# Linear attention in a five-stage network: scores within halves of 64 tokens, a state per half, weighted sums as one run of 64-row tiles

## What is computed

```python
q = softplus(x @ Wq.T + bq); k = softplus(x @ Wk.T + bk); v = x @ Wv.T + bv   # 16 heads of width 8
kv = cumsum(k[:, :, :, None] * v[:, :, None, :], axis=1)    # over the tokens
k1 = cumsum(k, axis=1)
num = einsum('zsD,zsDe->zse', q, kv);  den = sum(q * k1, axis=-1)
out = (num / den) @ Wo.T + bo
```

## Time and profile before

| what | value |
|---|---|
| three runs | 1309.18, 1315.74, 1320.01 us; median 1315.74 |
| span of the profiled execution, first to last instruction | 1294.8 us |
| the runs above this span | by 14.4 to 25.2 us (the profiled execution has no time of its own beside its span) |
| busy, share of the span | PE 83%, ACT 62%, DVE 50%, PEld 39%, POOL 29% |
| the linear stage | from the first scores at 844.9 us to the first expert loads at 1090.9 us |

### The profile page before, as it was taken

How to read it: one execution, slowest core, us unless ns; L and a number is a source line. 1 busy time by engine, 2 the same in 40 slices (tenths; PEclk the granted TensorE clock), 3 DMA queues, 4 the chain that set the end, 5 groups by cost and what they waited for, 6 DMA issues and landing times. The chain is left out here.

```text
span 1294.8 us, 21020 instructions
## 1 busy us (share of the span) xinstructions
PE 1070.8 (83%) x7616; PEld 500.4 (39%) x7616; DVE 653.5 (50%) x2099; ACT 807.3 (62%) x1164; POOL 373.6 (29%) x376
## 2 busy tenths in 40 slices
PE   4479998999999999999978858888877986998940
PEld 3242222322222231232256535534544554665620
DVE  5762555366356332333156326657867684633522
ACT  4348787877898989999934525555544441464520
POOL 2100110211110102333010664144331165265435
PEclk8679998999999999999998979989888897998975
DMA  5270370027028500300011323200000011233422
GB/s 144 55 105 1 58 101 2 1 41 106 14 42 120 157 1 15 114 17 18 19 38 49 104 83 94 68 17 20 15 14 5 1 34 58 72 109 110 133 66 67
DMA packets 83796, 74.08 MB, mean 57 GB/s; under 512 B 11440, under 2 KB 77872, under 8 KB 82800
## 3 DMA queue, kind: packets, MB, share of 16 engines
q1 hardware_dynamic: 73900, 54.93, 19.2%
q0 software_dynamic: 8192, 16.79, 4.4%
q10 hardware_dynamic: 1604, 0.99, 0.3%
HBM read 39.26 MB, written 33.42 MB: 56 GB/s over the span
## 5 line engine op out<-in xcount | busy, mean ns | idle before, releaser
L1275 ACT ACTIVATE attn_probs<-ps 128x1024 f32<-128x1024 f32 x512 | 485.5, 1072 | 73.1 <-PE ps L986 73.0
L1003 PE MATMUL ps<-attn_probs,attn_v 128*18 128x512 f32 x2048 | 274.9, 610 | 6.3 <-DVE room L1234 5.6
L1641 POOL DMA_INDIRECT slots<-moe_xr,moe_slot x128 | 124.8, 975 | 184.4 <-ACT attn_probs L1275 82.7
L986 PE MATMUL ps<-stack 50*128 50x512 bf16 x1024 | 166.2, 389 | 7.2 <-issue 1.2
L1651 POOL DMA_INDIRECT moe_back<-results,moe_slot x128 | 123.3, 963 | 115.2 <-PE ps L1696 45.4
L1706 PE MATMUL ps<-stack,lin_scores 128*128 x312 | 153.1, 613 | 0.0
L1807 ACT ACTIVATE lin_scores<-ps 128x256 f32<-128x256 f32 x156 | 58.5, 382 | 114.9 <-PE ps L1706 114.8
L986 PEld LDWEIGHTS ps<-stack 50*128 50x128 bf16 x1024 | 34.0, 94 | 244.1 <-ACT attn_probs L1275 229.3
L1780 DVE TENSOR_TENSOR lin_scores<-ps,lin_scores 128x256 f32<-128x256 f32 x156 | 59.1, 419 | 104.6 <-ACT lin_scores L1807 104.5
L1732 PE MATMUL ps<-stack,lin_scores 128*128 x624 | 85.1, 280 | 4.8 <-ACT lin_heads_out L1820 4.8
L1732 PEld LDWEIGHTS ps<-stack,lin_scores 128*128 128x128 f32 x624 | 77.4, 195 | 6.5 <-issue 6.5
(11 more groups left out here) (237 smaller groups left out, 1552.1 us busy)
## 6 DMA issues: line engine op xcount, KB each, us to landing
moe_gathered<-slots SPq DMA_DIRECT2D x76, 128.0 KB, 2.3
results<-lin_heads_out SPq DMA_DIRECT2D x76, 128.0 KB
stack<-qk_parts SPq DMA_DIRECT2D x36, 256.0 KB, 8.9
slots<-zeros SPq DMA_DIRECT2D x2, 2496.0 KB, 15.2
qk_parts<-moe_xr SPq DMA_DIRECT2D x32, 128.0 KB, 2.7
qk_parts<-moe_xr SPq DMA_DIRECT2D x16, 192.0 KB, 2.8
stack<-in_expert_w SPq DMA_DIRECT2D x1, 3072.0 KB, 10.4
stack<-qk_parts SPq DMA_DIRECT2D x12, 192.0 KB, 10.6
```

The source lines that it names most:

```text
L986: instruction = T.matmul(k.ps[:, SCORE_BANKS[i % 3][s], :], d.stack[b % 2][rows, 1, pair, kt * P:(kt + 1) * P], d.stack[b % 2][rows, 0, pa ...
L1003: instruction = T.matmul(k.ps[32 * j:32 * j + STRIP, PV_BANK, :], d.v[:, b % 2, kt, first:first + STRIP], d.probs[:, n % A_PROBS, j * BANK ...
L1275: A.activation(d.probs[:, n % A_PROBS, 2 * e * BANK:2 * (e + 1) * BANK], k.ps[:, banks[0]:banks[1] + 1, :].rearrange("p a n -> p (a n)"), ...
L1641: G.indirect_dma_start(out=k.dram["slots"][half], out_offset=bass.IndirectOffsetOnAxis(ap=d.slot[:, s, at, c:c + 1], axis=0), in_=d.xr[:, ...
```

## The change

Each chunk is cut into two halves s = 0, 1 of 64 tokens. Scores are made within a half only: 64 x 64 for a head, 256 columns for a head group, eight matmuls in place of four, each in a tile of 32 rows by 64 columns. The product that hides the later tokens has 256 columns. DVE reads the two banks 0 and 1 by one instruction, ACT the banks 2 and 3 by one. Each half needs its own state before it: `lstate` sums k x (v, 1) over the tokens 0 to 63 and over all 128 of the chunk, for all 32 chunks, DVE adds the total of the chunk before to both, and POOL spreads both to 288 columns. In `ldiv` the product with the state becomes two, one for each half, with a row of zeros in the first half of a sequence. The weighted sums of a chunk are 32 matmuls of 9 x 64 in tiles of 64 rows by 32 columns, in one run; half s writes bank 4 + s, and one ACT instruction copies both. `ldiv` comes two steps after them.

```diff
@@ plan_linear @@
-            if gr == HEAD_GROUPS - 1 and (u + 1) % TPB:
-                state = ("lstate", u)
+            if gr == 0:
+                state = ("lstate", g * TPG + c)
...
-        if n >= L_LAG and L_STEPS[n - L_LAG][2] == HEAD_GROUPS - 1:
+        if n >= L_LAG and n % HEAD_GROUPS == 0:
             sums = (n - L_LAG) // HEAD_GROUPS
-            works.insert(0, list(linear_finish(sums)))
+        if n >= L_LAG and n % HEAD_GROUPS == DIVIDE_AT:
+            works.insert(0, list(linear_finish((n - L_LAG) // HEAD_GROUPS)))
@@ pe_linear_side, lstate @@
+            for s, tokens in enumerate((slice(0, SUB), slice(0, P))):
+                for gr in range(HEAD_GROUPS):
+                    rows, heads = slice(32 * gr, 32 * (gr + 1)), slice(gr * HPG, (gr + 1) * HPG)
+                    instruction = T.matmul(k.ps[rows, bank, s * HPG * VW:(s + 1) * HPG * VW], d.k_tok[tokens, gg % NQ, c, rows],
...
@@ pe_linear_side, ldiv @@
+            T.wait_ge(k.l_state, u + 1)
+            for s in range(2):
...
+                instruction = T.matmul(k.ps[s * SUB:(s + 1) * SUB, bank, 0:HEADS * VW], d.q[:, gg % NQ, at:at + SUB], before,
+                                       start=True, stop=False)
@@ pe_linear, scores @@
+        for gr in range(HEAD_GROUPS // 2, HEAD_GROUPS):
+            T.matmul(k.ps[:, gr, 0:SUB_SCORES], d.hide[:, :], d.later[:, :, :].rearrange("p j t -> p (j t)"), start=True,
+                     stop=False)
         for gr in range(HEAD_GROUPS):
             rows = slice(32 * gr, 32 * (gr + 1))
-            T.matmul(k.ps[:, gr, :], d.k[rows, g % NQ, tokens],
-                     d.qz[rows, g % NQ, c, :, :].rearrange("p j t -> p (j t)"), start=not gr % 2,
-                     stop=True).then_inc(k.full[gr], 1)
+            for s in range(2):
+                at = c * P + s * SUB
+                instruction = T.matmul(k.ps[s * SUB:(s + 1) * SUB, gr, 0:SUB_SCORES], d.k[rows, g % NQ, at:at + SUB],
+                                       d.qz[rows, g % NQ, 2 * c + s, :, :].rearrange("p j t -> p (j t)"),
+                                       start=gr < HEAD_GROUPS // 2, stop=True)
+        instruction.then_inc(k.l_scored, 1)
@@ pe_linear, weighted_sums @@
-        for j in range(HPG):
-            instruction = T.matmul(out[PAD * j:PAD * j + VW, :], d.v[:, g % NQ, c, gr * HPG + j, :],
-                                   d.scores[:, n % NS, j * P:(j + 1) * P], start=True, stop=True)
+        for gr in range(HEAD_GROUPS):
+            for j in range(HPG):
+                for s in range(2):
+                    rows = slice(s * SUB, (s + 1) * SUB)
+                    instruction = T.matmul(k.ps[PAD * j:PAD * j + VW, L_OUT[s], gr * SUB:(gr + 1) * SUB],
+                                           d.v[rows, g % NQ, c, gr * HPG + j, :],
+                                           score_rows(d, u)[rows, gr, j * SUB:(j + 1) * SUB], start=True, stop=True)
         instruction.then_inc(k.l_av, 1)
@@ pool_linear_side, lstate @@
+            G.tensor_tensor(d.state[:, u % NST, :, :].rearrange("p s (g n) -> p s g n", g=HEAD_GROUPS),
+                            d.total[:, u % NST, :, :][:, :, None, :].broadcast_to(spread_to),
...
```

More of the change, by code:

```diff
@@ L415, in plan_linear @@
                 before.append(("lnorm", prepared + 1))
-            u = g * TPG + c
-            u = g * TPG + c
-            if gr == HEAD_GROUPS - 1 and (u + 1) % TPB:
-                state = ("lstate", u)
+            if gr == 0:
+                state = ("lstate", g * TPG + c)
         fill(before)
-        if n < len(L_STEPS) and gr == 0:
-            for i in range(HEAD_GROUPS):
-                k.banks.fill(("lscore", n + i), i)
         if state:
@@ L1994, in take, with scores @@
         return pe_take(T, k, key)
-    def scores(n, g, c):
+    def scores(u):
+        g, c = divmod(u, TPG)
         if c == 0:
@@ L2000, in scores @@
             T.wait_ge(k.l_masked[1], g + 1)
-        tokens = slice(c * P, (c + 1) * P)
-        for gr in range(HEAD_GROUPS):
-            bank = take(("lscore", n + gr))
-            if gr % 2:
-                T.matmul(k.ps[:, bank, :], d.hide[:, :], d.later[:, :, :].rearrange("p j t -> p (j t)"), start=True,
-                         stop=False)
+        if u:
+            T.wait_ge(k.l_read[0], u)
+            T.wait_ge(k.l_read[1], u)
+        for gr in range(HEAD_GROUPS // 2, HEAD_GROUPS):
+            T.matmul(k.ps[:, gr, 0:SUB_SCORES], d.hide[:, :], d.later[:, :, :].rearrange("p j t -> p (j t)"), start=True,
+                     stop=False)
@@ L2028, in pe_linear @@
     T.wait_ge(k.l_v_one, 1)
+    for bank in range(HEAD_GROUPS):
+        T.wait_ge(k.free[bank], k.banks.after["loop1"][bank])
     for piece in k.l_first:
@@ L2035, in pe_linear @@
         if n < len(L_STEPS) and n % HEAD_GROUPS == 0:
-            scores(n, *L_STEPS[n][:2])
+            scores(n // HEAD_GROUPS)
+        if k.l_sums[n] is not None:
+            weighted_sums(k.l_sums[n])
         if state:
@@ L2204, in act_linear @@
             side(piece)
-        for m in (n + 1, n + 3) if n < len(L_STEPS) and n % HEAD_GROUPS == 0 else ():
-            bank, fill = k.use["lscore", m]
-            A.wait_ge(k.full[bank], fill + 1)
-            A.activation(d.scores[:, m % NS, :], k.ps[:, bank, :], ACT_FN.Relu).then_inc(k.free[bank], 1)
+        if n < len(L_STEPS) and n % HEAD_GROUPS == 0:
+            u = n // HEAD_GROUPS
+            A.wait_ge(k.l_scored, u + 1)
+            A.activation(score_rows(d, u)[:, 2:4, :], k.ps[:, 2:4, 0:SUB_SCORES], ACT_FN.Relu).then_inc(k.l_read[1], 1)
+        if k.l_sums[n] is not None:
+            u = k.l_sums[n]
+            A.wait_ge(k.l_av, u + 1)
+            A.activation(d.sums[:, u % 2, :].rearrange("p (g s t) -> p s g t", g=HEAD_GROUPS, s=2),
+                         k.ps[:, L_OUT[0]:L_OUT[1] + 1, 0:SUB_SCORES].rearrange("p s (g t) -> p s g t", g=HEAD_GROUPS),
+                         ACT_FN.Copy).then_inc(k.l_sums_out, 1)
         for piece in after:
```

107 lines of the change are left out of this document (53 added, 54 removed).

## The result

The changed kernel takes 1310.8 us, median of 17 runs (1303.6 to 1313.0), beside 1315.9 for the kernel before, median of 17 timed beside it: ratio 0.9956, 95% interval 0.9942 to 0.9971. The forecast was 1297, a gain of 18.7 us; the measured gain is 5 to 6. Sign right, size wrong by 13 us. The profiled execution took 1303.6 us, with a span of 1301.8; so a run's time is its span and 1.8 us. That alone says something of the profile of before: its span of 1294.8 belongs to an execution of 1296.6 us, 19 us under the median beside it and under every one of the 17. The profiled execution of the changed kernel is also the fastest of its 17, 7 us under their median, so a difference of two spans is not the gain of the medians.

The account below looks back on a forecast made before the run. PE was taken to set the pace before the scatters and POOL after; 7.87 - 1.11 + 0.4 = 7.16 us a chunk gives -21.3 us, POOL +3.1, together -18, so 1297 us against 1315.7; eight-in-ten range 1283 to 1320.

Parts of the forecast that it names:

- the last one 53 us later: Predicted sign in the linear stage: first scatter near 1018 instead of 1039.8, last scatter 53 us after it.
- Rival C: PE in the linear stage: instructions don't come fast enough at 118 records a chunk; some +58 us, 1374 us; chance 5%.
- The sign by which I would call the forecast wrong: First scatter later than 1030, or second stretch over 6 us longer because POOL waits for late totals.
- Weighted sums: PE, first stretch: 64 records with row halves side by side take 0.7 us for 1.53, -0.83 us a chunk.
- Scores: PE, first stretch: 256 columns in eight tiles take 0.81 us for 1.29, -0.48 us a chunk.
- The state: PE, first stretch: two runs of 64 and 128 rows, the second waiting for the first, +0.28 us a chunk.
- item 7: PE, first stretch: new waits for ACT's copies before ldiv, lz and lproj, less old waits, net +0.4 us a chunk.
- rival E: PE idles more, so its clock falls to 0.80 and work costs 0.6 us more a chunk; 1312 us; chance 5%.
- Item 8: POOL, second stretch: seven state products of 288 columns at 0.87 us for six of 144, +3.1 us.
- Rivals A: PE's two halves take turns instead of running together, so the work hardly falls; 1318 us; chance 15%.
- B (a least time of 25 ns a record): Each PE record holds the array 25 ns, so weighted sums cost +0.32 us a chunk; 1316 to 1325 us; chance 7%.
- D (the new waits at +1.1): PE, first stretch: new waits and DVE's bursts eat the gain, +1.1 us a chunk; 1315 us; chance 15%.

Follow-up runs that it names:

- e14: The changed kernel, unedited, profiled again on a chip where the kernel before takes 1295.38 us: 1286.94 us (one run).
- e16: The changed kernel, unedited, on a chip where the kernel before takes 1298.98 us: 1278.82 us, ratio 0.9844 to before.
- e1: The kernel before, unedited, profiled once more: 1321.65 us, span 1319.8.
- e6: The changed kernel with three extra dense products of 256 columns ahead of each of PE's waits: 1307.80 us, ratio 0.9919 to before.
- e12: The kernel before with three extra dense products of 256 columns ahead of the same PE waits: 1320.88 us, ratio 0.9994 to before.
- e13: The changed kernel with four small 64-column products in place of each large one of e6: 1289.45 us, ratio 0.9942 to before.
- e17: The kernel of e6 (changed, three extra products ahead of PE's waits) timed on the chip of e16: 1271.02 us, ratio 0.9794 to before.
- e8: The kernel before with each hiding product made twice: 1316.96 us, ratio 0.9977 to before.
- e4: The changed kernel with all 32 scatters moved behind the linear stage: 1332.79 us, ratio 1.0100 to before.
- e11: The changed kernel with the edits of e6 and e4 together, three extra products and scatters behind the stage: 1329.31 us (one run).
- e15: The kernel before, unedited, profiled a third time, on the chip of e14: 1295.38 us (one run).
- e3: The changed kernel with only 17 of the 32 weighted-sum matmuls of a chunk: 1330.75 us, ratio 1.0088 to before.
- e7: The changed kernel with one dense 256-column product behind each of the first three groups of a weighted-sums run: 1323.11 us, ratio 1.0025 to before.

## Why the prediction was wrong, step by step

Parts of the span, us (A and B: the kinds of chips; e14 has 177.6 in stretch one, otherwise the parts of e16):

| | before, B | change, B (e16) | before, A (e1) | change, A |
|---|---|---|---|---|
| up to the stage | 844.9 | 842.7 | 846.3 | 840.7 |
| stretch one | 194.9 | 174.4 | 195.1 | 181.2 |
| stretch two | 48.8 | 53.4 | 60.6 | 65.1 |
| tail | 4.3 | 4.8 | 8.3 | 9.1 |
| the rest | 201.8 | 203.5 | 209.5 | 205.7 |
| span | 1294.8 | 1278.8 | 1319.8 | 1301.8 |

The stage itself (both stretches and the tail) falls from 248.0 to 232.6 us on B and from 264.0 to 255.4 on A: 15.4 and 8.6. The spans on A differ by 18.0 us where the medians differ by 5; 9.4 of the 18.0 lie outside the stage, which the change doesn't touch. So the columns for A show where the stage's time goes, not what the kernel gains.

**The step that failed** is the last one, "nothing outside the span changes, so against the median of 1315.7 it is 1297 us". It took the 14 to 25 us between the profile and the runs for a constant. A run is 1.8 us longer than its span; the rest was another kind of chip, where the stage has another balance: on A PE's instructions come late beside POOL's indirect DMAs, and for that the sum has no term. The sum is nearly right for the kind of chip that the trace came from: forecast 173.6 us for stretch one, measured 174.4 and 177.6; forecast "the last one 53 us later", measured 53.4. The ratio there is 0.9844 (one run of the change on the other B chip, beside the median of eight of before: 0.9933); I had 1297 / 1315.7 = 0.9858.

On A the change gets 7 us less in stretch one. L2033 there has 26.0 us of work and 5.4 of idle time, in e16 22.6 and 0.0: 8.8 us. **Rival C** asked for this with the wrong test. I bounded the supply of PE's instructions by a mean, 57 to 80 ns a record over a long stretch, and by nine records in 0.3 us, all from a B chip. What fails on A is the burst: after some 30 records in 0.3 us the rest of a run drips. The kernel before has no such run in stretch one, where its 32 records start over 0.79 us and the stretch takes 195.1 us on A and 194.9 on B. Beside the scatters it isn't spared: its stretch two is 11.8 us longer on A than on B, that of the change 11.7. So stretch two grows by 4.6 us on B and by 4.5 on A, and the 16 us between the first two profiles were the chip for the most part. The sign by which I would call the forecast wrong, POOL's waits for totals, is there on A with 12.5 us, but before has 7.0 of them on A too.

**The terms**, from e16 (lines of PE in stretch one), each against its share in the earlier trace rows:

```profile
L1972 PE MATMUL ps<-c_head_rows,lin_sums 128*128 128x36 f32 x192 | 31.0, 314 | 0.4 <-ACT lin_sums L2227 0.3
L2033 PE MATMUL ps<-lin_scores,lin_v 64*9 64x64 f32 x1536 | 22.6, 243 | 0.0
L1928 PE MATMUL ps<-room,c_lin_w 128*128 128x512 f32 x26 | 22.1, 944 | 6.8 <-DVE lin_total L2104 3.2 <-ACT room L2175 3.1 <-DVE lin_heads_out L2113 0.5
L2015 PE MATMUL ps<-lin_q_masked,lin_k 32*64 32x256 f32 x402 | 21.3, 479 | 0.0
L1948 PE MATMUL ps<-lin_v,lin_k_tok 64*32 64x36 f32 (+1 forms) x400 | 13.9, 222 | 2.0 <-DVE lin_heads_out L2113 2.0
```

1. Weighted sums: 22.6 / 24 = 0.94 us a chunk for 1.53, -0.58 where I had -0.83. The mechanism holds: the two row halves run together. The run needs 0.6 us to its last start and 0.25 behind it at the full clock, 0.8 at the low one; I had 0.44 and 0.25.
2. Scores: 21.3 / 25.1 = 0.85 for 1.29, -0.44 (forecast -0.48). The hiding product 11.7 us for 51 records, -0.27 (forecast -0.21).
3. The state: 13.9 / 25 = 0.56 for 0.23 over all chunks, +0.32 (forecast +0.28). Its product with q is 12.6 us, and 1.4 more with the row of zeros: 0.58 for 0.47, +0.11 (forecast +0.13).
4. The new waits, item 7: PE's idle time is 24.1 us in 24.25 chunks, 0.99 each; it was 30.9 in 24.75, 1.25. So -0.26 where I had +0.4. The new waits come (3.1 us on ACT for lz, none worth a line for ldiv), but the old ones shrink: the largest are for DVE's totals and heads, and DVE is busy 130 us for 137.
5. Not in my sum: the clock. L1972 and L1928, which the change does not touch, go from 280 to 314 and from 720 to 944 ns a record. Their rows in stretch one of the first profile, under the lines that they had there:

```profile
L1969 PE MATMUL ps<-c_head_rows,lin_sums 128*128 128x36 f32 x188 | 24.9, 280 | 0.9 <-DVE lin_total L2089 0.9
...
L1933 PE MATMUL ps<-room,c_lin_w 128*128 128x512 f32 x26 | 16.5, 720 | 2.0 <-ACT room L2160 1.6 <-DVE lin_heads_out L2098 0.2
```

 These two alone are 31.0 / 24 - 24.9 / 23.5 and 22.1 / 24.25 - 16.5 / 24.75, together +0.48 us a chunk. This is **rival E**, to which I gave 5%: I wrote 0.80 for its clock and 1312 for its time, and the runs show 0.80 and 1310.8, but the agreement in time is chance, since on B the clock is 0.81 and the gain 20 us. E's reason isn't borne out either: it had PE idle more, and PE is idle 14% of stretch one in e16 for 16% before. e6 beside e12 shows stretch one with the clock held in both: 19.4 us between them, on A.

The sum of 1 to 3 is -0.86 where I had -1.11, the waits are -0.26, the clock +0.48, and all other lines of PE -0.05: 194.9 / 24.75 = 7.87 becomes 174.4 / 24.25 = 7.19, where I had 7.16. That this is so near is luck: the waits came out 0.66 better than forecast, the terms 0.25 worse, and the clock and the other lines, for which I had nothing, 0.43 worse.

Item 8, POOL's state products, is right: 5.9 us for seven, forecast 6.1.

Rivals A (halves take turns) and B (a least time of 25 ns a record) are out: 64 records start in 0.60 us. D (the new waits at +1.1) is out by item 4. The Trainium skill's 60 cycles of overhead for each matmul (TensorEngine Tiling (Array Packing), Instruction Overhead) don't add up across tiles that run side by side; the row at 902.56 speaks against it.

On the clock: PE is busy 84% of stretch one in the first profile at 0.89, 86% in e16 at 0.81, 89% in e13 at 0.84 and 89% in e6 at 0.95. The Trainium skill, in TensorE: Matmul & The Clock Gate, Part 1, says that the clock is gated by how busy PE has been. If the busy share of the profile were meant, e16 and e13 should be granted more than before. They are not; a share of busy time in the rows does not foretell the level. With large products in the waits the clock rose from 0.80 to 0.95 (e6), with small ones from 0.80 in e14 to 0.84. Why is not settled by these runs.

Left open: why A and B chips differ; what POOL's indirect DMAs and PE's instructions share; how the 5 us between the medians on A divide into the stage's 8.6 and the rest; why the rest of the span, untouched by the change, is 202 to 205 us on B and 204 to 211 on A; and the 6.3 us between the spans of e14 and e16, 3.0 of them ahead of the stage and 3.2 in stretch one.

## What to carry to other kernels

A profile and a median from different chips must not be joined by a constant: set the span of the profiled execution against the runs first (here a run is its span and 1.8 us), and where they don't meet, the balance of engines in that profile is not that of the runs. Here smaller matmuls brought together took work from PE, but also clock and the slack for instructions; cost the lines that the change does not touch at the clock that they will get. A few large throwaway products can be worth more than they cost, if they cost PE little and lift its clock: in PE's waits 8 us on a B chip in the changed kernel (e17), but nothing in the kernel before (e12), which gained 3 us from doubled products on PE's path (e8).

## What the runs showed of the hardware

- Row halves and column tiles run at once: 64 records of 64 columns start 9.4 ns apart at the full clock, 12.5 at the low one (0.79 us).
- On A chips PE issues some 30 such records and then three to seven every 0.7 us, at times 1.4, while POOL's indirect DMAs run: in the changed kernel's profile the 15 runs with such a DMA in their first 0.6 us, and no other. Without them (e4, e11), and on B chips with them (e14, e16), no run takes over 0.95 us to its last start. The kernel before is held too: its stretch two is 60.6 us (e1) for 48.8 (e15).
- Taking work out of PE can make a kernel slower: e3, 731 records fewer, 1.0088 of before, at a clock of 0.63 (0.89 before).
- Adding work can make it faster: e8 0.9977, e6 0.9919 beside 0.9956, e17 0.9794 beside 0.9844.
- A large product between runs of small tiles costs 0.30 us at the full clock, for 0.107 us of columns (e7).
